# Cross-attention and FFN kernel: DVE takes over PSUM copies from ACT in the last three score steps of each block

## The reference

```python
kv_c = kv @ W_kvc;  q_c = layernorm(x) @ W_dq
scores = (q_nope . k_nope + rope(q_rope) . rope(k_rope)) * scale
good = (k_ids <= seg_id) & (k_ids >= seg_id - 8)
attn = softmax(where(good, scores, -1e30));  x = x + (attn @ v) @ W_o
g, u = (xn @ gate_w.T) * gate_s, (xn @ up_w.T) * up_s     # xn = layernorm(x)
out = x + ((silu(g) * u) @ down_w.T) * down_s
```

## Time and profile before

| | |
|---|---|
| three runs | 779.44 us median (776.15 to 779.57) |
| profiled execution | 781.95 us, its span 780.2 us |
| mean granted clock of TensorE | 0.986 of full speed |
| PE busy | 733.5 us (94% of the span) |
| DVE busy | 452.6 us (58%) |
| ACT busy | 408.0 us (52%) |

### The profile page before, as it was taken

How to read it: one execution, slowest core, us unless ns; L and a number is a source line. 1 busy time by engine, 2 the same in 40 slices (tenths; PEclk the granted TensorE clock), 3 DMA queues, 4 the chain that set the end, 5 groups by cost and what they waited for, 6 DMA issues and landing times.

```text
span 780.2 us, 18039 instructions
## 1 busy us (share of the span) xinstructions
PE 733.5 (94%) x7102; PEld 687.7 (88%) x7102; DVE 452.6 (58%) x944; ACT 408.0 (52%) x899; POOL 198.0 (25%) x330
## 2 busy tenths in 40 slices
PE   4989789989998999999998999989999999999997
PEld 4878669779987999779987999779999999999997
DVE  2889845755567356745666547846682453636242
ACT  4878635664457445664467445756676232323231
POOL 1656652614053402604063404330000000000000
PEclk9999979999999999999999999989999999999999
DMA  8899964054313432144303432074201202021011
GB/s 282 254 345 305 300 197 104 11 132 89 87 36 106 90 80 68 33 108 91 90 28 112 89 76 70 4 283 196 68 1 34 69 1 80 21 67 34 28 58 34
DMA packets 46358, 81.19 MB, mean 104 GB/s; under 512 B 5483, under 2 KB 30107, under 8 KB 46283
## 3 DMA queue, kind: packets, MB, share of 16 engines
q1 hardware_dynamic: 40796, 53.67, 25.9%
q0 software_dynamic: 5488, 26.50, 10.0%
HBM read 57.26 MB, written 11.28 MB: 88 GB/s over the span
## 4 chain that ended last, share of the span: by engine, by line
PE 77%; DVE 9%; ACT 5%; DMA 5%; issue 2%; POOL 1%; SPq 0%; DVEq 0%; POOLq 0%
PE ps L1405 18%; PE ps L1108 12%; PE ps L971 11%; PE ps L1437 9%; PE ps L1113 6%; PE ps L1046 4%; PE ps L186 3%; PE ps L1019 3%; DMA ctx_raw<-ctxT_dram 2%; DMA kv_table<-tab 2%; ACT q_lat L1151 2%; PE ps L981 2%; PE ps L1010 2%; PE ps L1035 1%; DVE prob_wide L1248 1%
## 5 line engine op out<-in xcount | busy, mean ns | idle before, releaser
L1258 DVE TENSOR_TENSOR o_lo<-q_lat,o_hi 128x320 fp32r<-128x320 f32 x80 | 69.8, 880 | 82.9 <-ACT o_hi L1159 79.6
L1108 PE MATMUL ps<-o_hi,wvo_hi 128*128 128x320 f32 x320 | 97.5, 315 | 1.8 <-ACT o_hi L1159 1.8
L1159 ACT ACTIVATE o_hi<-q_lat 128x320 fp32r<-128x320 f32 x80 | 65.9, 830 | 62.9 <-PE ps L1108 61.9
L1108 PE MATMUL ps<-o_hi,wvo_lo 128*128 128x320 f32 x320 | 96.4, 312 | 0.0
L1489 ACT ACTIVATE silu<-ps,ffn_scale 128x320 f32<-128x320 f32 x55 | 29.0, 527 | 97.5 <-PE ps L1405 97.5
L910 POOL TENSOR_TENSOR rot_c<-gathered,cosq 128x192 f32<-128x192 f32 x40 | 25.0, 624 | 167.7 <-PE ps L981 149.3
L1540 DVE SCALAR_TENSOR_TENSOR hidden<-ps,ffn_scale,silu 128x320 f32<-128x320 f32 x55 | 30.2, 549 | 60.5 <-ACT silu L1489 52.8
L1108 PEld LDWEIGHTS ps<-o_hi,wvo_hi 128*128 128x128 f32 x320 | 61.2, 191 | 2.3 <-ACT o_hi L1159 2.0
L1108 PEld LDWEIGHTS ps<-o_hi,wvo_lo 128*128 128x128 f32 x320 | 61.1, 191 | 0.3
L1113 PE MATMUL ps<-o_lo,wvo_hi 128*128 128x320 f32 x320 | 60.4, 310 | 0.0
L524 PE MATMUL ps<-wkv,ctx_hi 128*128 128x384 f32 x192 | 54.5, 395 | 5.0 <-ACT ctx_hi L386 5.0
(11 more groups left out here) (171 smaller groups left out, 1878.5 us busy)
## 6 DMA issues: line engine op xcount, KB each, us to landing
ctx_raw<-ctxT_dram SPq DMA_DIRECT2D x16, 722.0 KB, 7.9
gathered<-key_rows SPq DMA_DIRECT2D x240, 47.2 KB
head_w<-head_w_dram SPq DMA_DIRECT2D x16, 576.0 KB, 5.4
ffn_raw<-ffn_w_dram POOLq DMA_DIRECT2D x11, 768.0 KB, 12.9
kv_table<-tab POOLq DMA_DIRECT2D x16, 288.0 KB, 6.8
rows<-x_dram SPq DMA_DIRECT2D x5, 640.0 KB, 5.2
residual<-x_dram SPq DMA_DIRECT2D x20, 160.0 KB, 2.4
x_rows<-residual SPq DMA_DIRECT2D x20, 160.0 KB, 2.0
```

Of the source, the lines that this page charges most:

```text
L1108: last = pe.matmul(ps[:, 4 + m, 0:TB], w[wt][:, h, cols], o_hi[h % 2][:, :], start=(h == 0 and n == 0), stop=False, skip_group_check=True)
L1159: act.activation(o_hi[h % 2][:, :], q_lat[:, h % 2, :, h // 2], ACT.Copy).then_inc(oh_ok, 1)
L1258: dve.tensor_tensor(o_lo[h % 2][:, :], q_lat[:, h % 2, :, h // 2], o_hi[h % 2][:, :].bitcast(F32), ALU.subtract).then_inc(ol_ok, 1)
```

## The change

Two kinds of copies from PSUM change their engine. In steps 5, 6 and 7 of every block, the copy of side 1 of the values is made by DVE (`take_second_values`) in place of ACT; ACT still makes side 0, and DVE waits for it by `lat_ev`. In blocks 0 to 3, the four copies of turned rows into `rowsT` (steps 5 and 6) are made by DVE (`high_by_vector`) in place of ACT. In all, 15 value copies and 16 row copies move. No shape, bank or semaphore changes.

```diff
+SHARED_STEPS = (STEPS - 3, STEPS - 2, STEPS - 1)
...
+    def high_by_vector(self, dve, b, t, banks):
+        dve.wait_ge(self.turned, self.c4(b, t + 1))
+        dve.tensor_copy(self.t_hi[:, :, t * LT:(t + 1) * LT], self._bank(t, banks)).then_inc(self.hi_ok, 1)
...
         def take_values(b, s):
             act.wait_ge(av_mm, c8(b, s + 1))
-            for side in range(2):
+            for side in range(1 if s in SHARED_STEPS else 2):
                 if side:
                     act.wait_ge(lat_ev, c16(b, 2 * s + 1))
...
                 for t in tiles_at(s):
                     if last:
                         ln_f.high(act, 0, t, (2, 3))
-                    else:
-                        ln.high(act, b + 1, t, (2, 3))
...
+        def take_second_values(b, s):
+            dve.wait_ge(lat_ev, c16(b, 2 * s + 1))
+            dve.tensor_copy(side_tokens(s, 1), made_values(1)).then_inc(lat_ev, 1)
...
                 if NLT <= s + 1 < NLT + 3:
                     next_norm(b, last, s + 1)
-                if last:
-                    for t in tiles_at(s):
+                if s in SHARED_STEPS:
+                    take_second_values(b, s)
+                for t in tiles_at(s):
+                    if last:
                         ln_f.low(dve, 0, t, (2, 3))
+                    else:
+                        ln.high_by_vector(dve, b + 1, t, (2, 3))
```

More of the change, by code:

```diff
@@ L802, in side_tokens, with made_values @@
         return spans[:, :, :, at:at + GQ, :].rearrange("p g e t i -> p g e (t i)")
+    def made_values(side):
+        return ps[:, 6 + side, 0:GROUPS * SK].rearrange("p (g e r) -> p g e r", g=GROUPS, e=2)
     def turn_back(pe, b):
@@ L1147, in take_values @@
             act.wait_ge(av_mm, c8(b, s + 1))
-            for side in range(2):
+            for side in range(1 if s in SHARED_STEPS else 2):
                 if side:
                     act.wait_ge(lat_ev, c16(b, 2 * s + 1))
-                act.activation(
-                    side_tokens(s, side), ps[:, 6 + side, 0:GROUPS * SK].rearrange("p (g e r) -> p g e r", g=GROUPS, e=2),
-                    ACT.Copy).then_inc(lat_ev, 1)
+                act.activation(side_tokens(s, side), made_values(side), ACT.Copy).then_inc(lat_ev, 1)
         def high_latent(b, h):
```

## The result

| | before | with the change |
|---|---|---|
| runs | 776.93 us median (774.41 to 779.57, 6 runs) | 792.42 us median (790.37 to 794.09, 6 runs) |
| ratio, 95% interval | | 1.0198 (1.0168 to 1.0228) |
| profiled execution, span | 781.95, 780.2 us | 790.37, 788.6 us |
| mean granted clock | 0.986 | 0.971 |

The kernel became 2% slower, 15.5 us by the medians; the forecast was 5.5 us, and the time lies 3.9 us above the top of the range.

The account below looks back on a forecast made before the run. PE bounds the kernel, its chain running over ACT in the last score steps. Waits of 2.3 us plus clock falls of 3.2 us make 5.5, added to the 779.44 us median: 785.0 us, range 780.4 to 788.5.

Parts of the forecast that it names:

- What bounds the kernel; DVE is not free: Late score steps: PE's chain runs over ACT's copies, while DVE is normalising until 165.28 in block 0.
- Price of a moved value copy, 0.50 us: Side 1 value copy of 128x336 on DVE: 0.50 us, against 0.450 on ACT; bounds 0.45 and 0.82.
- Step 5, 0.91 us late: DVE's copy waits behind the normalisation, so `values(6)` starts 0.91 us later.
- step 6, 0.45 us: ACT saves 0.46 us of the 0.91 lost, so `values(7)` starts 0.45 us later; 1.80 us over blocks 0 to 3.
- The transposed rows cost nothing: Row copies moved to DVE in blocks 0 to 3 cost nothing, with 0.1 us to spare before `compress`.
- Block 4, 0.54 us: Last block, no `compress` to hide the last value copy: `o_hi` starts 0.54 us late.
- The clock: Blocks 0 to 3: longer PE gap makes the clock fall three times instead of once, 1.6 us each, 3.2 us.
- The waits: PE's waits for the moved copies: 1.80 us in blocks 0 to 3 plus 0.54 in block 4, 2.3 us.
- The full bound: Upper bound of the clock's term: all four of blocks 0 to 3 fall, 4.9 us.
- Rule on micro-idles: Skill page: micro-idles between matmul groups can make the clock go back and forth; every block would fall, 4.9 us.
- Rival 3: Steps 5 and 6: DVE copies as soon as side 0 is there, `values(7)` 0.89 us early; 775.0 us, chance 0.05.

Follow-up runs that it names:

- filled form: Changed kernel with unread 128x320 matmuls in PE's gaps (9 before `values(6)`, 1 before `values(7)`, 13 after it in block 4), against the kernel before: 0.999.
- second pair: Kernel before and changed kernel, both unchanged, profiled again on one chip: 1.001 and 1.0191 against the kernel before.
- early form: Changed kernel with DVE's value copy placed ahead of the normalisation, against the kernel before: 0.9987, 778.7 us.
- dose: Changed kernel with 3 or 6 unread matmuls before `values(6)` and none elsewhere, against the kernel before: 1.0115 and 1.004.
- the full and the small work: Changed kernel with 8 unread 128x320 matmuls, or 24 unread 56x56 transposes, behind the unchanged gap, against the kernel before: 1.0133 and 1.0308.
- e5_before_filled: Kernel before with unread matmuls in PE's gaps (4 before `values(6)`, 4 before `values(7)`, 10 after it in block 4), against the kernel before: 0.9971.

## Why the prediction was wrong

- *What bounds the kernel; DVE is not free.* Right: the gap before `values(6)` is released by DVE, 1.79 us.
- *Price of a moved value copy, 0.50 us.* Measured 0.50 and 0.51. What the Trainium skill says of ScalarE and PSUM (VectorE: DVE Perf Modes, Specifications) agrees with this trace by 0.05 us a copy, and that explains none of the 2%.
- *Step 5, 0.91 us late; step 6, 0.45 us.* Right in size, 0.49 us per block where the clock held (filled form). In the changed kernel itself step 6 did not come about: with PE at 1.2 GHz `values(7)` follows without waiting.
- *The transposed rows cost nothing.* Right, 0.9995.
- *Block 4, 0.54 us.* From the start of the normalisation to the first head it took 6.07 us before and 7.34 after. The wait is in it; the remaining 0.7 us are the last values product, 1.65 us at 1.2 GHz instead of 0.95.
- *The clock: "I take three falls in blocks 0 to 3 instead of one: 2 x 1.6 = 3.2 us".* This is the step that failed, in both of its factors. All four blocks fell, in both profiles of the changed kernel, where the second profile of before has no fall in them. And the price of 1.6 us came from a block in which PE went from `values(7)` straight into `compress`. In the changed kernel the fall comes one step earlier, in front of transposes and values products, and lasts twice as long: of the 3.31 us per block, 0.49 are the wait and 2.8 the clock. Four blocks by 3.3 us are 13.2; the second pair is 14.9 us apart in all, which leaves 1.7 us for block 4 and the rest. The waits are 4 x 0.49 + 0.54 = 2.5 us of this, so the clock's term, forecast at 3.2 us, measured about 12.4. The full bound that the text gave for this term, 4.9 us, used the wrong price too, so the range could not hold the time. The prediction had a better price in its own rows: in block 4, behind the only gap of 1.8 us, two heads took 6.27 us instead of 3.52, 2.75 us more. Four falls at that price less the one that before had are 4 x 2.75 - 1.6 = 9.4 us, and with the waits 791.1 us.
- *Rule on micro-idles (the Trainium skill, TensorE: Matmul & The Clock Gate, section on the second HAM failure mode).* As the prediction read it, it spoke for a fall in every block. This case agrees for the gap of 1.79 us, with four falls in four blocks, and mostly not for the gaps of 0.8 us, with one in four and then none in the two profiles of before. Priced at 1.6 us it would still have missed.
- *Rival 3.* Its mechanism exists when the order in DVE's queue is changed, but it was worth some 1 us, not 4.4: the early form still waits 0.88 us for the copy, and SP's queue takes part of the rest back. With SP's queue out of the way it was 0.37 us a block.

That the late copy's gap makes the clock fall, and that the fall is the larger part of the cost, was shown by the earlier copy, by filling and by dose. That the work behind the gap changes whether and for how long it falls was shown by the full and the small work, in one profile each. What sets the length of one fall, and why the hole in step 4 comes and goes, stays open.

## What to carry to other kernels

Before a copy moves to an engine that is idle on average, read what stands ahead of it in that engine's queue at that moment: one place in DVE's queue made the difference between 1.0198 and 0.9987. Price a gap on TensorE by the clock too, and take the price from a place where the same kind of work follows; where a gap can't be closed, a few full matmuls that nobody reads can be cheaper than the fall, as they were here. When an edit on the critical path brings less than it should, look for the queue that was hidden just behind it, here SP's.

## What was not expected of the hardware

- PE, busy all the time, ran on at a granted clock of 0.50 for 7 us in each of blocks 0 to 3, in block 0 the first 4 us of it with small matmuls and transposes and the rest in `compress`; with 24 transposes more it was 10 us in two of them. Eight full 128x320 matmuls behind the same 1.8 us gap avoided the fall in two blocks of four.
- Adding work to PE did not cost time but seems to have saved some: 1.0198 became 1.0133 with eight more matmuls per block, at a place where PE waits for nothing. From `compress` of block 0 to that of block 1, where the fall was avoided, PE's timeline shows 86.45 us (171.57 to 258.02) against 87.99 (170.77 to 258.76) in the second profile of the changed kernel.
- The kernel before had medians of 776.6 to 779.8 us in five sets of runs. In the set beside e5_before_filled its executions ran from 772.92 us (mean clock 0.998) to 781.24 us (0.983): most of the spread goes with the clock.
